# The residual of a graph convolution as a fourth filter, taken out of PSUM by VectorE

## The chip, the cores and the metric

The kernel runs on one core of a Trainium2 chip. The metric is the time of one execution on the device, in microseconds (us). TensorE (PE) multiplies, VectorE (DVE), ScalarE (ACT) and GpSimd (POOL) work elementwise, and SyncE (SP) issues the transfers. Each engine works its own queue in the order in which it is written; semaphores tie the queues together. Products land in PSUM, which has 8 banks of 128 partitions x 512 floats.

## The reference

The input is x, 16 batches x 256 nodes x 16 features x 16 time steps. A graph convolution with temporal and spatial attention comes first, then a linear attention layer, then a mixture of experts. The change lies in the end of the first block:

```
out = zeros
for k in range(3):
    r = einsum('mn,bmn,bmft->bnft', cheb[k], S, x)
    out = out + einsum('bnft,fo->bnot', r, Theta[k])
sg = relu(out)
tc = conv(sg, tw, kernel 1x3, pad 1) + tb        # over the time steps
res = einsum('bnft,of->bnot', x, rw) + rb
y = relu(res + tc)
y = (y - mean(y)) / sqrt(var(y) + 1e-5) * gamma + beta
```

S is a softmax that depends on the batch. Since the filters Theta work on the features only, the kernel applies them first, to x, and mixes the nodes afterwards.

## The kernel before

The batches go through in 8 pairs. Each pair runs through chains of named steps: `conv` (the graph convolution), `tail` (its normalisation), `attn`, `route` and `ffn` (the experts, 12 steps of a pair: gu, h, dn, w). One list, PROGRAM, puts the steps of all pairs in one order, and every engine issues its part of each step in that order (`run`). The list is written out by hand: OPENING for the pairs 0 to 2 of `conv`, BODY once per turn for the pairs 3 to 7, CLOSING for the end. In the list `+n` means n steps of the experts, which are to keep TensorE busy. `hot` steps are products whose result nobody uses; they fill gaps in the opening. `high` and `low` steps split the weights, on ScalarE and on VectorE.

The products of conv and attn land in a ring of four banks. Tile i of the whole list takes bank i % 4, and TensorE waits (`wait_bank`) until the tile four places before it was read out; READ_OUT says by which instruction of which engine.

The steps around the change, for a pair p and a batch b of it:
- xT: x, normalised and transposed, kept in `xT` (features and times on the partitions). M, prod, Epre, Eexp, Erep, lr, p2, sp, rv, st: the two attentions of the graph part. VectorE has small instructions in most of them; prod's is `te` (L931), ScalarE's tanh on it is L745, and Epre (L1304) needs that.
- Y0, Y1 (`filter_products`, L1237): strips of 32 rows of `xT` against the three filters, 16 products of 96 columns into four banks. ScalarE copies each bank to `y_s` (L740); that copy frees the bank.
- st (L1345), o0, o1 (L1355): transposes of the softmax, VectorE's products with cheb (L994), then the mixing of the nodes. ScalarE takes the relu to `sg` (L771).
- tc0, tc1: the bias as a product of `ones` and `bias_hl` (L1368), four residual products of `xT` with `residual_s` (L1373), four products of the time convolution with `tconv_s` (L1374, L1375). ScalarE takes the relu to `kept` (L776).
- z1: sums (L999), mean off (L1002), squares on ScalarE, products with gamma on GpSimd; z2: sums of squares, L1010, and three Newton steps on VectorE; z3: the rest.
- gn: statistics of x (L895) and one product (L1268).
- lg, r1 to r4, cb: the choice of experts. r4 is L1173 to L1181 on VectorE; cb (L1471) transposes its result, which then goes through DRAM to the experts.

In VectorE's queue the steps of BODY around Y0 read h, Y0, silu, r4, prod, cb, and around Y1 out0, V01, w, S10, Y1, h, st1, o0, o1, tc0, tc1, z1. In OPENING they read `0:M 0:Y0 2:gn 1:M`, then `0:Eexp 1:Y0 1:prod 2:xg`, then `0:tc1 0:high3 2:Y0 0:z1 1:rv1 2:prod 0:z2 0:low1 1:Y1 1:st1`.

Of the kernel before, what the change touches and what calls it, by code (L numbers as in the profile page):

```python
# [12 lines left out]
P = 128  # L13
B = 16
N = 256
T = 16
# [203 lines left out]
def graph_attention_moe(nc, x, out, small, consts, cheb, theta, residual, tconv, vsT, bsT, wqkvT, woT, gateT, upT, down):  # L220
    x_v = x.rearrange("(p b) (c n) f t -> p b n c (f t)", b=2, n=P)
    out_v = out.rearrange("(p b) (c n) f t -> p b n c (f t)", b=2, n=P)
    with ExitStack() as ctx:
# [17 lines left out]
        theta_s = sb("theta_s", [P, 3, 2, T])  # L241
        residual_s = sb("residual_s", [P, T, 8])
        tconv_s = sb("tconv_s", [P, T, 10])
        bias = sb("bias", [P, T])
        bias_h = sb("bias_h", [P, T], F32R)
        bias_hl = sb("bias_hl", [P, T], F32R)
# [11 lines left out]
        ones = sb("ones", [P, P], F32R)  # L258
# [158 lines left out]
        def fill(p, name):  # L417
# [4 lines left out]
            "M": "um sums left0 right1 left1", "prod": "te", "Epre": "emax esub", "Eexp": "e1 e2 e3 e4 e5 esum erec ET", "Erep": "EW WE", "p2": "pb0 pb1",  # L422
# [46 lines left out]
        for b in BI:  # L469
            READ_OUT["xT" + b] = [(conv_act, "xT" + b)]  # L470
            READ_OUT["p2_" + b] = [(conv_dve, "pb" + b)]
            READ_OUT["sp" + b] = [(conv_act, f"ex{b}1")]
            READ_OUT["st" + b] = [(conv_dve, f"A{b}2")]
            READ_OUT["o" + b] = [(conv_act, "sg" + b)]
            READ_OUT["tc" + b] = [(conv_act, "relu" + b)]
            READ_OUT["tok" + b] = [(attn_act, f"nm{2 * int(b) + 1}")]
            READ_OUT["tk" + b] = [(route_act, f"nm{2 * int(b) + 1}")]
            READ_OUT["xl" + b] = [(attn_dve, "lo" + b)]
            READ_OUT["xn" + b] = [(route_dve, "lo" + b)]
            READ_OUT["q" + b] = [(attn_dve, "q" + b)]  # L480
# [81 lines left out]
        PREP_POOL = 11  # L562
# [4 lines left out]
        def _(sp):  # L567
# [11 lines left out]
            sp.dma_start(residual_s[:, :, :], residual).then_inc(load["blocks"], 16)  # L579
# [65 lines left out]
        def _(pool):  # L645
# [4 lines left out]
            pool.memset(bias_hl[:, :].bitcast(F32), 0.0).then_inc(prep_pool, 1)  # L650
# [53 lines left out]
        def _(act):  # L704
# [11 lines left out]
            def front(p, name):  # L716
# [5 lines left out]
                if t is not None:  # L722
                    act_reads = name in ("xT0", "xT1", "lr", "o0", "o1", "tc0", "tc1", "xl0", "xl1", "xn0", "xn1", "kt", "q0", "q1", "k0", "k1", "v0", "v1")
                    if act_reads:
                        act.wait_ge(*filled_at(p, name))
                if name == "M" and p == 0:
                    act.wait_ge(prep_dve, 6)
                    act.wait_ge(prep_pool, 6)
                    act.activation(bias_h[:, :], bias[:, :], ACT.Copy).then_inc(prep_act, 1)
                    act.activation(bias_hl[64:65, :], bias[64:65, :], ACT.Copy).then_inc(prep_act, 1)  # L730
# [110 lines left out]
        def _(dve):  # L841
            def prepare():

                dve.wait_ge(load["small"], 16)
                dve.wait_ge(load["first"], 16)
                dve.tensor_scalar(ve_h[:, :, :], small_at("ve", T).unsqueeze(1).to_broadcast([T, 4, T]), 0.5, None, ALU.mult).then_inc(prep_dve, 1)
                dve.tensor_copy(iw1[:, 0:16], const_at("ident", T)[:, 0:16]).then_inc(prep_dve, 1)
                dve.tensor_copy(iw1[:, 16:17], small_at("w1", T)).then_inc(prep_dve, 1)
                dve.tensor_copy(iw1[:, 17:18], small_at("w1", T)).then_inc(prep_dve, 1)
                dve.wait_ge(prep_act, 1)  # L850
                dve.tensor_tensor(router[:, :, 1, :], small_at("router").rearrange("p (k e) -> p k e", k=2), router[:, :, 0, :].bitcast(F32), ALU.subtract).then_inc(prep_dve, 1)
                dve.tensor_tensor(bias[:, :], small_at("tb"), small_at("rb"), ALU.add).then_inc(prep_dve, 1)
                dve.tensor_scalar(ones[:, :], ident, 0.0, 1.0, ALU.mult, ALU.add).then_inc(prep_dve, 1)
# [28 lines left out]
            def front(p, name):  # L882
# [80 lines left out]
                if name == "lr" and p == 0:  # L963

                    dve.wait_ge(load["rest"], 16)
                    dve.wait_ge(prep_act, 3)
                    dve.wait_ge(prep_dve, 6)
                    dve.tensor_tensor(bias_hl[96:97, :], bias[96:97, :], bias_h[96:97, :].bitcast(F32), ALU.subtract).then_inc(prep_dve, 1)
# [238 lines left out]
        def _(pe):  # L1207
# [19 lines left out]
            def filter_products(p, name):  # L1227
# [29 lines left out]
            def front(p, name):  # L1257
# [32 lines left out]
                if name in ("Y0", "Y1"):  # L1290
                    if p == 0:
                        pe.wait_ge(load["blocks"], 48)
# [38 lines left out]
                if name in ("sp0", "sp1"):  # L1331
                    b = int(name[2])
                    if p == 0:
                        pe.wait_ge(prep_dve, 9)
# [25 lines left out]
                if name in ("tc0", "tc1"):  # L1360

                    b = int(name[2])
                    if p == 0:
                        pe.wait_ge(prep_dve, 8)
                        pe.wait_ge(prep_pool, 6)
# [224 lines left out]
```

## Time and profile before

| | |
|---|---|
| median of 3 runs | 949.14 us (947.37 to 950.04) |
| span of the profiled execution, first to last instruction | 943.2 us |
| TensorE busy | 896.8 us |
| VectorE busy | 604.5 us |
| ScalarE busy | 426.2 us |
| GpSimd busy | 210.3 us |

The profile is of one execution. Its own time is its span; the runs' times have some microseconds around the span (949.14 - 943.2 = 5.9). A step's busy time says nothing of whether it delays the end: for that one reads who waits for whom.

### The profile page before, as it was taken

Reading aid. Unit: us, or ns where it says so; the run is one execution under the profiler, and the core shown is the slowest. Engines: PE = TensorE matmul, PEld = TensorE weight load, DVE = VectorE, ACT = ScalarE, POOL = GpSimd, SP = SyncE. Lnnn points to the kernel's source line nnn. Section 1 sums busy time; section 2 is a strip of 40 time slices with the busy share of each in tenths; the row PEclk is TensorE's granted clock in tenths of the full one; section 3 lists DMA queues with packets and bytes.
Section 4 is the critical chain, followed back from the end, with each engine's and each line's share of the span. In section 5 each row is a group of like instructions: output and inputs, shape, how many; then the busy total and the mean of one; then the engine's idle time right before and its main releaser. Section 6 shows DMA issues by size and latency. Waiting matters only on the chain.

```text
span 943.2 us, 19688 instructions
## 1 busy us (share of the span) xinstructions
PE 896.8 (95%) x8000; PEld 799.1 (85%) x8000; DVE 604.5 (64%) x1615; ACT 426.2 (45%) x781; POOL 210.3 (22%) x183
## 2 busy tenths in 40 slices
PE   4898879999999999999999999999999999999997
PEld 3687658998988998898988989888888898988997
DVE  6637967677775379654786458853787537764522
ACT  2534534831674336552464425652366424622442
POOL 2004101233301142112411124021331123122232
PEclk9999999999999999999999999999999999999998
DMA  6000400111011100210002010020001100020121
GB/s 233 2 1 1 171 23 2 57 62 35 13 39 57 35 24 13 73 35 23 24 14 82 24 35 23 25 72 31 27 13 52 55 2 24 30 77 24 38 66 34
DMA packets 36249, 39.26 MB, mean 42 GB/s; under 512 B 3392, under 2 KB 32576, under 8 KB 36160
## 3 DMA queue, kind: packets, MB, share of 16 engines
q1 hardware_dynamic: 36160, 38.01, 12.7%
q8 instruction: 64, 1.05, 0.5%
q14 instruction: 25, 0.20, 0.1%
HBM read 33.02 MB, written 4.98 MB: 40 GB/s over the span
## 4 chain that ended last, share of the span: by engine, by line
PE 85%; DVE 6%; DMA 4%; ACT 2%; issue 2%; POOL 1%; SPq 0%; POOLq 0%; DVEq 0%
PE ring L1355 9%; PE d_ps L521 5%; PE g_ps L521 5%; PE d_ps L522 4%; PE d_ps L523 4%; PE g_ps L523 4%; PE g_ps L522 4%; PE u_ps L522 4%; PE u_ps L521 4%; PE u_ps L523 4%; PE ring L1223 4%; PE num L1252 3%; PE ring L1338 3%; PE ring L1455 3%; PE ring L521 3%; PE ring L523 2%
## 5 line engine op out<-in xcount | busy, mean ns | idle before, releaser
L699 POOL TENSOR_TENSOR hl<-hb,hh 128x512 fp32r<-128x512 f32 x96 | 126.7, 1320 | 480.0 <-ACT hh L836 480.0
L836 ACT ACTIVATE hh<-hb 128x512 fp32r<-128x512 f32 x96 | 60.6, 632 | 181.8 <-DVE hb L1195 169.4
L521 PE MATMUL d_ps<-hh,down_h 128*128 128x256 f32 x384 | 114.9, 299 | 5.1 <-POOL hl L699 5.1
L521 PE MATMUL g_ps<-normed_h,gate_h 128*128 128x256 f32 x352 | 107.4, 305 | 3.5 <-DVE hb L1190 3.5
L1190 DVE TENSOR_TENSOR hb<-sl,u_ps 128x512 f32<-128x512 f32 x88 | 60.2, 684 | 77.2 <-PE u_ps L523 35.9
L522 PE MATMUL d_ps<-hl,down_h 128*128 128x256 f32 x384 | 107.7, 280 | 0.0
L523 PE MATMUL d_ps<-hh,down_l 128*128 128x256 f32 x384 | 107.7, 280 | 0.0
L522 PE MATMUL g_ps<-normed_l,gate_h 128*128 128x256 f32 x352 | 99.8, 283 | 0.0
L523 PE MATMUL g_ps<-normed_h,gate_l 128*128 128x256 f32 x352 | 99.8, 283 | 0.0
L522 PE MATMUL u_ps<-normed_l,up_h 128*128 128x256 f32 x352 | 99.5, 283 | 0.0
L521 PE MATMUL u_ps<-normed_h,up_h 128*128 128x256 f32 x352 | 99.4, 283 | 0.0
L523 PE MATMUL u_ps<-normed_h,up_l 128*128 128x256 f32 x352 | 99.4, 282 | 0.0
L1082 DVE TENSOR_TENSOR shared<-ring,constants 128x512 f32<-128x512 f32 x128 | 79.4, 683 | 16.4 <-PE ring L1223 16.4
L521 PEld LDWEIGHTS d_ps<-hh,down_h 128*128 128x128 f32 x384 | 72.5, 189 | 16.5 <-POOL hl L699 8.2
L521 PEld LDWEIGHTS g_ps<-normed_h,gate_h 128*128 128x128 f32 x352 | 67.0, 190 | 13.3 <-issue 8.1
L522 PEld LDWEIGHTS d_ps<-hl,down_h 128*128 128x128 f32 x384 | 72.8, 190 | 0.4 <-issue 0.2
L523 PEld LDWEIGHTS d_ps<-hh,down_l 128*128 128x128 f32 x384 | 72.6, 189 | 0.0
L833 ACT ACTIVATE sl<-g_ps 128x512 f32<-128x512 f32 x88 | 52.7, 599 | 41.5 <-PE g_ps L523 41.2
L522 PEld LDWEIGHTS g_ps<-normed_l,gate_h 128*128 128x128 f32 x352 | 67.1, 191 | 1.5 <-issue 1.2
L523 PEld LDWEIGHTS g_ps<-normed_h,gate_l 128*128 128x128 f32 x352 | 67.0, 190 | 0.0
L521 PEld LDWEIGHTS u_ps<-normed_h,up_h 128*128 128x128 f32 x352 | 66.7, 189 | 0.0
L522 PEld LDWEIGHTS u_ps<-normed_l,up_h 128*128 128x128 f32 x352 | 66.6, 189 | 0.0
(413 smaller groups left out, 2092.5 us busy)
## 6 DMA issues: line engine op xcount, KB each, us to landing
weights_over_hidden<-weights_by_expert SPq DMA_DIRECT2D x128, 128.0 KB, 2.9
shared<-denominators_by_head SPq DMA_DIRECT2D x16, 256.0 KB
out_x<-kept SPq DMA_DIRECT2D x16, 256.0 KB, 2.2
x_s<-in_x SPq DMA_DIRECT2D x12, 256.0 KB, 3.6
raw_weights<-in_gateT SPq DMA_DIRECT2D x4, 384.0 KB, 6.6
raw_weights<-in_upT SPq DMA_DIRECT2D x4, 384.0 KB, 6.0
raw_weights<-in_down SPq DMA_DIRECT2D x4, 384.0 KB, 8.0
cheb_s<-in_cheb SPq DMA_DIRECT2D x3, 256.0 KB, 4.9
```

The costliest lines, as they stand in the source:

```text
L521: eng.matmul(ps, wh, xh, start=start, stop=False, **how)
L522: eng.matmul(ps, wh, xl, start=False, stop=False, **how)
L523: return eng.matmul(ps, wl, xh, start=False, stop=stop, **how)
L699: pool.tensor_tensor(hl[:, j % 2, :], hb, hh[:, j % 2, :].bitcast(F32), ALU.subtract).then_inc(*ffn_pool.mark(p, f"lo{j}"))
L833: act.activation(sl, gate_up(p, j)[0][:, :], ACT.Silu).then_inc(*ffn_act.mark(p, f"si{j}"))
L836: act.activation(hh[:, j % 2, :], hb, ACT.Copy).then_inc(*ffn_act.mark(p, f"hi{j}"))
L1082: dve.tensor_tensor(p_s[:, j, :].rearrange("p (h l) -> p h l", h=4), tile(p, n)[:, :].rearrange("p (h l) -> p h l", h=4), const_at("causal ...
L1190: dve.tensor_tensor(hb, sl, gate_up(p, j)[1][:, :], ALU.mult).then_inc(*ffn_dve.mark(p, f"h{j}"))
L1223: last = pe.matmul(tile(p, n)[:, 2 * c * P:(2 * c + 2) * P], k_f[rows, c, cols], q_eo[rows, :, c, cols], start=True, stop=True, tile_posit ...
L1252: last = pe.matmul(num[rows, c * L + lc * P:c * L + lc * P + P], v_s[:, b, lc, 4 * c + j, 16 * odd:16 * odd + 32], p_s[:, j, (2 * c + odd) ...
L1338: last = pe.matmul(t[:, kc * N:(kc + 1) * N], vs_s[:, jc, kc * P:(kc + 1) * P], g.th[:, b, jc, :], start=(jc == 0), stop=(jc == 1))
L1355: last = pe.matmul(t[:, c * N:(c + 1) * N], g.y_s[b][:, m, c, k], g.a_s[:, k, m, :], start=(k == 0 and m == 0 and c == 0), stop=(k == 2 an ...
```

## The change

The residual's weights become a fourth filter of the strip product, which now fills its four banks completely (128 columns per product). ScalarE still copies the three filters' parts of a bank to `y_s`. Behind it VectorE takes the fourth part, adds the bias and writes it to `kept`; that take frees the bank. The bias product and the residual products of tc go. VectorE adds what it kept to the bank of tc, in place, ahead of ScalarE's relu. The wait for the stored output of three pairs before moves from the relu to the first take. Some preparation goes: one transfer, a memset, two copies, two VectorE instructions.

```
-        theta_s = sb("theta_s", [P, 3, 2, T])
-        residual_s = sb("residual_s", [P, T, 8])
+        theta_s = sb("theta_s", [P, 4, 2, T])
...
-                READ_OUT[f"Y{b}_{j}"] = [(conv_act, f"y{b}{j}")]
+                READ_OUT[f"Y{b}_{j}"] = [(conv_dve, f"r{b}{j}")]
...
-                        act.activation(g.y_s[b].rearrange("p m c k s -> p (m c k) s")[:, :, 32 * j:32 * j + 32],
-                                       tile(p, n)[:, 0:384].rearrange("p (q s) -> p q s", s=32), ACT.Copy).then_inc(*conv_act.mark(p, f"y{b}{j}"))
+                        act.activation(g.y_s[b].rearrange("p m c k s -> p (m c) k s")[:, :, :, 32 * j:32 * j + 32],
+                                       tile(p, n)[:, :].rearrange("p (q k s) -> p q k s", k=4, s=32)[:, :, 0:3, :], ACT.Copy).then_inc(*conv_act.mark(p, f"y{b}{j}"))
...
                 if name in ("tc0", "tc1"):
                     b = int(name[2])
-                    if p >= 3:
-                        act.wait_ge(out_stored[p % 3], 32 * (p // 3))
+                    act.wait_ge(conv_dve.of(p), conv_dve.at(p, f"res{b}"))
                     act.activation(x1_at(p)[:, :, b, :], t[:, :].rearrange("p (m r) -> p m r", m=2), ACT.Relu).then_inc(*conv_act.mark(p, f"relu{b}"))
...
+                if name in ("Y0", "Y1"):
+                    b = int(name[1])
+                    if p == 0 and not b:
+                        dve.wait_ge(prep_dve, 6)
+                    if p >= 3:
+                        dve.wait_ge(out_stored[p % 3], 32 * (p // 3))
+                    for j, n in enumerate(banks_of(name)):
+                        dve.wait_ge(conv_act.of(p), conv_act.at(p, f"y{b}{j}"))
+                        by_k = tile(p, n)[:, :].rearrange("p (m c k s) -> p m c k s", m=2, c=2, k=4)
+                        dve.tensor_tensor(x1_at(p)[:, :, b, :].rearrange("p m (c s) -> p m c s", c=2)[:, :, :, 32 * j:32 * j + 32], by_k[:, :, :, 3, :],
+                                          bias[:, :, :].rearrange("p t o -> p (t o)").unsqueeze(1).to_broadcast([P, 2, 2 * T]).unsqueeze(1).to_broadcast([P, 2, 2, 2 * T]),
+                                          ALU.add).then_inc(*cv.mark(p, f"r{b}{j}"))
+                if name in ("tc0", "tc1"):
+                    b = int(name[2])
+                    dve.wait_ge(*filled_at(p, name))
+                    own(cv, p, f"r{b}3")
+                    by_o = t[:, :].rearrange("p (m o t) -> p m o t", m=2, t=T)
+                    dve.tensor_tensor(by_o, by_o, x1_at(p)[:, :, b, :].rearrange("p m (t o) -> p m o t", o=T), ALU.add).then_inc(*cv.mark(p, f"res{b}"))
...
-                            last = pe.matmul(tile(p, n)[:, q * 96:(q + 1) * 96], g.xT[rows, b, c, m * P:(m + 1) * P],
+                            last = pe.matmul(tile(p, n)[:, q * P:(q + 1) * P], g.xT[rows, b, c, m * P:(m + 1) * P],
...
-                    pe.matmul(by_o, ones[:, :], bias_hl[:, :].unsqueeze(1).to_broadcast([P, 2, T]).unsqueeze(3).to_broadcast([P, 2, T, T]),
-                              start=True, stop=False, skip_group_check=True)
                     for m in range(2):
                         cols = slice(m * P, (m + 1) * P)
-                        for c in range(2):
-                            pe.matmul(by_o[:, m, :, 8 * c:8 * c + 8], g.xT[:, b, c, cols], residual_s[:, :, :], start=False, stop=False, skip_group_check=True)
-                        pe.matmul(by_o[:, m, :, 0:9], g.sg[:, b, 0, cols], tconv_s[:, :, 1:10], start=False, stop=False, skip_group_check=True)
+                        pe.matmul(by_o[:, m, :, 0:9], g.sg[:, b, 0, cols], tconv_s[:, :, 1:10], start=(m == 0), stop=False, skip_group_check=True)
```

## Rows read from the trace of the kernel before

**Rows 1.** Windows: engine busy us (instructions), granted clock, DMA share, GB/s.
```profile
25.00:50.00 25.00, 21.37 (x183) 15.71 (x182) 15.60 (x46) 14.33 (x36) 0.00 (x0) 0.93 0.01 2
...
440.00:560.00 120.00, 117.99 (x1076) 105.17 (x1073) 80.42 (x216) 54.52 (x100) 29.21 (x24) 1.00 0.11 33
```

**Rows 2.** Chain of waits, one turn: start us, us, engine, tile, line, count with loads.
```profile
420.36 1.08 PE ring L1237 x32
421.43 1.01 PE num L1252 x32
...
433.61 0.44 PE ring L1373 x4
```

**Rows 3.** Source line L1068: duration in ns, min/median/max.
```profile
L1068 DVE TENSOR_SCALAR one_over_denominator<-ring x8: 281/286/292, 111.4 to 827.6; 128x128 f32<-128x128 f32 x8
```

**Rows 4.** Timeline of tc0, tc1: start us, us, engine, line, tiles, [idle before].
```profile
433.04 0.57 PE L1368 MATMUL ring<-bias_hl,ones 128*128 128x512 f32 x1
...
433.43 0.60 ACT L771 ACTIVATE filters<-ring 128x512 f32<-128x512 f32 x1 [4.58 <-PE ring L1355]
...
433.45 0.61 PE L1373 MATMUL ring<-residual_s,first 128*128 128x128 f32 x4
...
437.31 0.38 PE L521 MATMUL d_ps<-hh,down_h 128*128 128x256 f32 x1
...
437.61 0.60 ACT L776 ACTIVATE kept<-ring 128x512 f32<-128x512 f32 x1 [1.49 <-PE ring L1375]
...
438.90 1.15 PE L1223 MATMUL ring<-shared 32*128 32x256 f32 x16
```

**Rows 5.** Timeline behind Y0 in a turn of BODY.
```profile
490.61 0.22 DVE L1173 SCALAR_TENSOR_TENSOR pairs<-emark,sc 128x64 f32<-128x64 f32 x1
...
490.70 1.64 ACT L740 ACTIVATE filters<-ring 128x384 f32<-128x384 f32 x4 [1.44 <-PE ring L1237]
...
491.54 0.22 DVE L1181 TENSOR_TENSOR pairs<-pairs,wsum 128x64 f32<-128x64 f32 x1
...
492.30 0.60 PE L1471 MATMUL num<-constants,pairs 128*16 128x128 f32 x4
...
492.41 0.18 DVE L931 TENSOR_TENSOR conv_small<-ring,small_parameters 16x32 f32<-16x32 f32 x1 [0.65 <-PE ring L1298]
...
492.99 0.27 PE L1304 MATMUL ring<-conv_small,ve_h 16*64 16x32 f32 x2
```

**Rows 6.** Timeline of the opening behind Y0 of pairs 0 and 1.
```profile
18.36 1.41 DVE L895 BATCH_NORM_STATS2 conv_small<-x_s 128x6 f32<-128x256 f32 x4
19.08 1.64 ACT L740 ACTIVATE shared<-ring 128x384 f32<-128x384 f32 x4 [0.51 <-PE ring L1237]
...
20.72 0.36 PE L1268 MATMUL ring<-conv_small,constants 128*128 128x8 f32 x2 [1.71 <-ACT shared L740]
...
26.70 1.64 ACT L740 ACTIVATE raw_weights<-ring 128x384 f32<-128x384 f32 x4 [0.78 <-PE ring L1237]
...
27.54 0.18 DVE L931 TENSOR_TENSOR sl<-ring,small_parameters 16x32 f32<-16x32 f32 x1
```

**Rows 7.** Timeline of the opening, z1 of pair 0 to st1 of pair 1.
```profile
67.32 1.48 DVE L999 TENSOR_REDUCE shared<-kept 128x32 f32<-128x512 f32 x2
...
72.92 1.06 DVE L1010 TENSOR_SCALAR shared<-shared 128x64 f32<-128x64 f32 x1
...
73.39 0.66 PE L1345 MATMUL ring<-constants,raw_weights 128*128 128x128 f32 x4 [0.30 <-ACT raw_weights L740]
...
76.69 0.95 DVE L859 TENSOR_TENSOR wqkv_l<-raw_weights,wqkv_h 128x768 fp32r<-128x768 f32 x1
```

**Rows 8.** Timeline of the opening, Erep of pair 2.
```profile
91.49 1.06 PE L1311 MATMUL ring<-iw,first 16*128 16x17 f32 x8 [1.60 <-ACT shared L791]
```

**Rows 9.** Windows around a fall of the granted clock.
```profile
106.00:108.00 2.00, 0.69 (x5) 0.52 (x6) 1.93 (x4) 1.15 (x2) 0.00 (x0) 1.00 0.81 306
...
110.00:112.00 2.00, 2.00 (x20) 1.28 (x20) 1.65 (x4) 2.00 (x4) 0.00 (x0) 0.50 1.04 395
```

More of the change, by code:

```diff
@@ L217, with graph_attention_moe @@
 PLACE = {f: i for i, f in enumerate(FILLS)}
-def graph_attention_moe(nc, x, out, small, consts, cheb, theta, residual, tconv, vsT, bsT, wqkvT, woT, gateT, upT, down):
+def graph_attention_moe(nc, x, out, small, consts, cheb, theta, tconv, vsT, bsT, wqkvT, woT, gateT, upT, down):
     x_v = x.rearrange("(p b) (c n) f t -> p b n c (f t)", b=2, n=P)
@@ L240, in graph_attention_moe @@
         cheb_s = sb("cheb_s", [P, 3, 2, N])
-        theta_s = sb("theta_s", [P, 3, 2, T])
-        residual_s = sb("residual_s", [P, T, 8])
+        theta_s = sb("theta_s", [P, 4, 2, T])
         tconv_s = sb("tconv_s", [P, T, 10])
-        bias = sb("bias", [P, T])
-        bias_h = sb("bias_h", [P, T], F32R)
-        bias_hl = sb("bias_hl", [P, T], F32R)
+        bias = sb("bias", [P, 2, T])
         vs_s = sb("vs_s", [P, 2, N])
@@ L257, in graph_attention_moe @@
         down_h = sb("down_h", [P, CHUNKS, N], F32R)
-        ones = sb("ones", [P, P], F32R)
         over = sb("weights_over_hidden", [P, 2, 512])
@@ L421, in graph_attention_moe @@
             "gn": "bn0 bn1 bn2 bn3 ag0 ag1 ag2 ag3 msq m2 gm gsq gvar", "xg": "xg0 xg1 xg2 xg3",
-            "M": "um sums left0 right1 left1", "prod": "te", "Epre": "emax esub", "Eexp": "e1 e2 e3 e4 e5 esum erec ET", "Erep": "EW WE", "p2": "pb0 pb1",
+            "M": "um sums left0 right1 left1", "prod": "te", "Epre": "emax esub", "Eexp": "e1 e2 e3 e4 e5 esum erec ET", "Erep": "EW WE", "p2": "pb0 pb1", "Y0": "r00 r01 r02 r03", "Y1": "r10 r11 r12 r13", "tc0": "res0", "tc1": "res1",
             "sp0": "smax0", "sp1": "smax1", "rv0": "rinv0", "rv1": "rinv1", "st0": "A00 A01 A02", "st1": "A10 A11 A12"}), early("conv_by_dve"))
@@ L561, in graph_attention_moe @@
         ROUTED_DOWN = {2: 13, 3: 14, 4: 14, 5: 14}
-        PREP_POOL = 11
+        PREP_POOL = 10
         assert len(PIECES) == len(CHAINS["high"]) == len(CHAINS["low"])
@@ L578, in _ @@
             sp.dma_start(theta_s[:, :, :, :], theta).then_inc(load["blocks"], 16)
-            sp.dma_start(residual_s[:, :, :], residual).then_inc(load["blocks"], 16)
             sp.dma_start(tconv_s[:, :, :], tconv).then_inc(load["blocks"], 16)
@@ L649, in _ @@
                 pool.memset(r.ab[:, :, :], 0.0).then_inc(prep_pool, 1)
-            pool.memset(bias_hl[:, :].bitcast(F32), 0.0).then_inc(prep_pool, 1)
             pool.memset(gs[:, :, :], FILLER).then_inc(prep_pool, 1)
@@ L722, in front @@
                 if t is not None:
-                    act_reads = name in ("xT0", "xT1", "lr", "o0", "o1", "tc0", "tc1", "xl0", "xl1", "xn0", "xn1", "kt", "q0", "q1", "k0", "k1", "v0", "v1")
+                    act_reads = name in ("xT0", "xT1", "lr", "o0", "o1", "xl0", "xl1", "xn0", "xn1", "kt", "q0", "q1", "k0", "k1", "v0", "v1")
                     if act_reads:
@@ L726, in front @@
                 if name == "M" and p == 0:
[L727 to L730, printed above, removed]
+                    act.wait_ge(prep_pool, 2)
                 if name in ("xT0", "xT1"):
@@ L851, in prepare @@
                 dve.tensor_tensor(router[:, :, 1, :], small_at("router").rearrange("p (k e) -> p k e", k=2), router[:, :, 0, :].bitcast(F32), ALU.subtract).then_inc(prep_dve, 1)
-                dve.tensor_tensor(bias[:, :], small_at("tb"), small_at("rb"), ALU.add).then_inc(prep_dve, 1)
-                dve.tensor_scalar(ones[:, :], ident, 0.0, 1.0, ALU.mult, ALU.add).then_inc(prep_dve, 1)
+                dve.tensor_tensor(bias[:, :, :], small_at("tb").unsqueeze(1).to_broadcast([P, 2, T]), small_at("rb").unsqueeze(1).to_broadcast([P, 2, T]),
+                                  ALU.add).then_inc(prep_dve, 1)
             def split(i):
@@ L965, in front @@
                     dve.wait_ge(load["rest"], 16)
-                    dve.wait_ge(prep_act, 3)
-                    dve.wait_ge(prep_dve, 6)
-                    dve.tensor_tensor(bias_hl[96:97, :], bias[96:97, :], bias_h[96:97, :].bitcast(F32), ALU.subtract).then_inc(prep_dve, 1)
                     dve.wait_ge(load["graph"], 96)
@@ L1291, in front @@
                     if p == 0:
-                        pe.wait_ge(load["blocks"], 48)
+                        pe.wait_ge(load["blocks"], 32)
                     pe.wait_ge(conv_act.of(p), conv_act.at(p, f"xT{name[1]}"))
@@ L1333, in front @@
                     if p == 0:
-                        pe.wait_ge(prep_dve, 9)
+                        pe.wait_ge(prep_dve, 7)
                     pe.wait_ge(conv_act.of(p), conv_act.at(p, f"th{b}"))
@@ L1563 @@
     consts = _np.concatenate([c[n].astype(f32) for n in CONST], axis=1)
-    theta = _np.zeros((8, T, 3, 2, T), f32)
-    residual = _np.zeros((8, T, T, 8), f32)
+    theta = _np.zeros((8, T, 4, 2, T), f32)
     tconv = _np.zeros((8, T, T, 10), f32)
     for t in range(8):
-        theta[t, :, :, t % 2, :] = a["L0_conv_Theta"].transpose(1, 0, 2)
-        residual[t, :, :, t] = a["L0_conv_rw"].T
+        theta[t, :, 0:3, t % 2, :] = a["L0_conv_Theta"].transpose(1, 0, 2)
+        theta[t, :, 3, t % 2, :] = a["L0_conv_rw"].T
         tconv[t, :, :, t:t + 3] = a["L0_conv_tw"][:, :, 0, ::-1].transpose(1, 0, 2)
-    theta, residual, tconv = (v.reshape((P,) + v.shape[2:]) for v in (theta, residual, tconv))
+    theta, tconv = (v.reshape((P,) + v.shape[2:]) for v in (theta, tconv))
     given = {
-        "x": a["x"], "small": small, "consts": consts, "cheb": a["L0_conv_cheb"], "theta": theta, "residual": residual, "tconv": tconv,
+        "x": a["x"], "small": small, "consts": consts, "cheb": a["L0_conv_cheb"], "theta": theta, "tconv": tconv,
         "vsT": a["L0_conv_V_s"].T, "bsT": a["L0_conv_b_s"][0].T,
```

3 lines of the change are left out of this document (removed).

## The prediction

> **What bounds the kernel now.** I read the page's busy times first (the table above): TensorE is busy nearly all the span, ScalarE and VectorE are far from it. The windows of the span then show that this is an average over two different kernels: between 440 and 560 us TensorE works 98% of the time (117.99 of 120 us), between 25 and 50 us only 85%, with VectorE at 15.60 of 25 [rows 1]. So in the steady part (pairs 3 to 7 of the graph stage, one each 111.12 us, five times) a microsecond taken off TensorE is a microsecond gained, unless TensorE then waits; in the opening (pairs 0 to 2) the end is set by chains that go from engine to engine in the order written in OPENING, and VectorE's place in them matters as much as its speed. Every engine works its queue in order, so a VectorE instruction that waits for ScalarE holds up everything written behind it. That is what I look for in the timelines [rows 5 to 8].
>
> **TensorE loses work in tc.** Per tc step the change takes away one 512-column bias product and four residual products, each of which is two passes; four passes last 0.44 us in the chain of waits [rows 2], so eight are 0.89. The pass behind the bias product starts 0.41 us after it [rows 4]; part of that is the end of the product before, which stays, so its share is between 0 and 0.41, and I take half, 0.21. Together 1.1 us a step, 2.2 us a pair, 17.6 us over 8 pairs. That is nearly the whole possible gain: of the preparation, a few small instructions on three engines and a transfer go, 0 to 0.5 us once, and I take 0.
>
> **The fourth filter on TensorE.** The strip product goes from 96 to 128 moving columns, in 8 groups of four side by side. Its step takes 1.08 us in the chain; the attention's weighting has the same 8 groups, 128 columns wide, and takes 1.01 [rows 2]. So 96 columns do not pay by the column today, and a residual pass with 128 weight columns and 128 moving ones takes 0.11, which is 0.89 for 8 [rows 2]. Bounds for the 16 steps: 0 below, 0.36 x 16 = 5.8 us above, if all 1.08 grew with the columns. I take 0, the nearest rows being those 128 wide.
>
> **ScalarE** still moves 384 elements of each bank, now in blocks of 96; four take 1.64 us today [rows 5]. No row has that pattern out of PSUM; the 128x512 eviction takes 0.60 [rows 4], which bounds the one of 384 from above: 0 to 0.1 more each, and I see no reason for a gain. I take 0.
>
> **VectorE gains** eight takes of 128 elements a pair (nearest: a 128x128 read of PSUM, 0.286 us median [rows 3]) and two adds of 512 (nearest: two reductions of 512 in 1.48, or 0.7 each [rows 7]; no row writes its result back to PSUM, so 0.6 to 1.0). That is 8 x 0.28 + 2 x 0.7 = 3.6 us a pair, 29 us in all. Its busy time allows for that. The question is what stands behind them. The wait for the stored output, which moves to the first take, costs nothing: the store of three pairs before is issued about a sixth of a turn ahead of Y0.
>
> **Steady part, Y0.** In VectorE's queue the order is h2, Y0, r4, prod. Today Y0 has nothing there: r4 (L1173 to L1181) starts at 490.61 and ends at 491.76, before TensorE wants its result for cb at 492.30 [rows 5]. ScalarE's four evictions run from 490.70 to 492.34. With the change the fourth take starts at 492.38 and ends at 492.66; r4 starts at about 492.60, which is 1.99 us later, and ends at 493.75. TensorE can start cb (L1471) at 493.80 instead of 492.30. The te addition (L931), 492.41 today, comes behind r4 at 493.76, the tanh follows, and Epre (L1304) is ready at about 494.33 instead of 492.99. So TensorE loses 1.35 us, and nothing filled that time for it. The weights' way through DRAM starts at cb and shifts with TensorE, so its stalls stay what they are. The same rows come back five times, first at 268 and last at 713 us.
>
> **Steady part, Y1.** Here the takes run while VectorE is idle. But the bank that st1 needs is free only after the first take, 0.3 us behind ScalarE, of which about 0.1 is covered: 0.2 us.
>
> **Steady part, tc.** o1 ends at 433.4, its relu at 434.03 [rows 4]. tc0 is then done at 434.2, so tc1 doesn't wait. Between tc and z1 comes a hop: product, add 0.7, relu 0.60. The relu of tc1 ends 1.5 us behind the last product where it is 0.9 today; S11 takes that bank 1.6 us behind it (437.31 to 438.90, [rows 4]), so it just fits. The sums and subtractions, the masks of S11 and V11 come 0.7 us later against TensorE, with slack of 0.8 to 0.9. I put 0.1 us here. A pair: -2.2 + 1.35 + 0.2 + 0.1 = -0.55; five pairs: **-2.7 us**.
>
> **Opening, Y0 of pairs 0 and 1.** In the queue of VectorE pair 2's statistics stand behind pair 0's Y0. They start at 18.36 today; ScalarE's evictions end at 20.72 [rows 6], so the last take ends at 21.03 and the statistics start at 20.96: 2.6 us later, and TensorE's next product (L1268, 20.72) waits for them. The row already shows TensorE idle there; it is the same chain, so nothing absorbs it. In pair 1, the te addition at 27.54 stands behind takes that end 0.3 us after 28.34 [rows 6]: 1.1 us more. Sum **+3.7**. Pair 0's Y1: as in the steady part, with nothing over it, **+0.3**.
>
> **Opening, 66 to 80 us.** This is the costly place. VectorE's queue reads: tc1 of 0, Y0 of 2, z1 of 0, rv1 of 1, prod of 2, z2 of 0, low1, Y1 of 1, st1 of 1. Today z1 starts at 67.32, and TensorE transposes st1 of 1 at 73.39, while z2 and low1 run on VectorE until 77.64 beside the next products [rows 7]. With the change:
> - tc0 and tc1 of pair 0 end earlier on TensorE, but st0 of 1 waits for ScalarE's scaling, and the relu of tc1 comes through VectorE: Y0 of 2 starts 0.2 us earlier, not 2.2.
> - z1 now stands behind the takes of Y0 of 2, which end at 71.15. It starts at 71.1 and ends at 73.8 (2.67 us, as today).
> - te of 2 ends at 74.1. The squares and GpSimd's two products come behind the subtractions; L1010, which today ends with GpSimd's second product (72.92 + 1.06 = 73.98, [rows 7]), ends at about 76.1.
> - From L1010's end to low1's end it is 3.66 us today (73.98 to 77.64): 79.8.
> - Only then comes the take of the first bank of Y1 of 1, which ends at 80.05. st1 uses that bank, so TensorE starts it at 80.1 where it was 73.39.
> That is **+6.7 us**, the 0.2 included. TensorE stands still for some 4 us of it. Today the eviction alone frees the bank; so the cover of z2 by o0 and o1 is lost.
>
> **Opening, the rest.** tc of 1: TensorE waits at Erep of 2 (L1311, 1.60 us idle today, [rows 8]) for a normalisation behind relu1 and shift; of 2.2 us I keep **-0.8**. Y1 of 2: **+0.3**. tc of 2: **-2.2**. Opening: 3.7 + 0.3 + 6.7 - 0.8 + 0.3 - 2.2 = **+8.0 us**.
>
> **The clock.** Today the granted clock is 1.00 at 106 to 108 us, while TensorE works 0.69 of 2 us, and 0.50 at 110 to 112 [rows 9]; between 25 and 50 us the mean is 0.93, which at 25 x 0.07 is 1.75 us of lost work in one fall to 1.2 GHz [rows 1]. The idle stretch of 4 us before st1 of pair 1, where the products of o0 run without a gap today, should bring one more: **+1.7 us** (bounds 0 and 3.4). The Trainium skill says the same in general (TensorE: Matmul & The Clock Gate, section on HAM oscillation): a wait that is long enough drops the array to half clock, and the loss is half of the throttled time. By that rule as well, one more fall costs 1.7; it speaks against this change, whose sum without it would be 5.3.
>
> **Sum** against the profiled span of 943.2 us: +8.0 - 2.7 + 1.7 = +7.0, so 950.2. The runs' median, 949.14, is 5.9 above the span, which I keep: **956 us**, 0.7% slower.
>
> **Rivals.**
> - *The opening gives most of it back.* If the stretch at 66 to 80 costs no more than the late normalising (1.5 us instead of 6.7) and the clock doesn't fall: 2.8 - 2.7 = 0, 949. For it: the opening has idle time on every engine. Against: the waits are in the order of the queues, which the diff doesn't touch. 0.18.
> - *TensorE's saving carries.* The other side: the bound is TensorE's work, and VectorE's takes are covered. Place: tc, 8 x 2.2 = 17.6 us. If nothing waits it is 931; it decides from the point where the waits of Y0, 1.35 each, and the opening's 11 us lose half, 940 to 946. For it: TensorE's 98% in the steady part [rows 1]. Against: r4 has 0.54 us of slack at cb, and comes 1.99 later [rows 5]. 0.12.
> - *VectorE and the columns cost more.* If the strip product pays by its columns (5.8 us), the takes in four-level patterns are slower or the clock falls twice: 962. For it: no row has these patterns. Against: 128 columns side by side take 1.01 us [rows 2], and the takes read rows of 32 neighbours. 0.10.
> - My forecast: 0.60, its own range 952 to 959.
>
> **How the numbers follow.** About 0.3%, or 2.8 us, is what a measurement of this kernel tells from no change. Slower: the forecast 0.60 and the last rival 0.10. Same: 0.18. Faster: 0.12. The range 946 to 963 leaves the saving that carries fully below and a double clock loss above.
>
> **What would show it.** After: L1173 starts behind the fourth take in every turn and TensorE idles 1.3 to 1.5 us at L1471 or Epre, the turn being 110.6 us instead of 111.12; in the opening the statistics of pair 2 start near 21.0, and TensorE idles at least 3 us before st1 of pair 1, near 84 us in the new trace, with z2 and low1 on VectorE. The steps are wrong if the strip product lasts over 1.2 us, if cb starts on time, or if st1 of 1 comes within 6 us of the old 73.4. If the turn is shorter than 110 us, the prediction is wrong about Y0.

## The result, and the profile after

| | before | after |
|---|---|---|
| median (runs) | 949.59 us (4; 947.37 to 950.96) | 957.25 us (4; 956.72 to 960.29) |
| span of the profiled execution | 943.2 us | 955.0 us |
| TensorE busy | 896.8 us | 891.2 us |
| VectorE busy | 604.5 us | 636.1 us |
| ScalarE busy | 426.2 us | 425.4 us |

The changed kernel is slower: ratio 1.0094, 95% interval 1.0069 to 1.0118. A second set, told below, gives 1.0085 (1.006 to 1.011). The forecast was 956, range 946 to 963. One execution of a later kernel took 1301 us at a mean granted clock of 0.64 and is left out of its numbers (experiment 6). TensorE is busy 5.6 us less, VectorE 32 us more, and the span is 11.8 us longer, so TensorE's idle time grew by 17.4 us. (TensorE's busy time shrinks by less than the work that was taken off it, since products last longer at the lower clock; see below.) The waits of TensorE, summed over the span after; the columns are the engine's group of products, what it waited for, us in total, times, longest:

```profile
PE num L1469 <- DVE pairs L1186: 7.0, 5, 1.4
...
PE ring L1273 <- DVE conv_small L894: 4.3, 1, 4.3
PE ring L1350 <- DVE kept L972: 3.5, 2, 3.2
...
PE ring L1316 <- ACT shared L781: 3.1, 1, 3.1
...
PE d_ps L517 <- POOL hl L693: 2.7, 2, 2.2
PE ring L1242 <- ACT kept L766: 2.6, 1, 2.6
PE ring L1242 <- DVE conv_small L921: 2.6, 1, 2.6
PE ring L1228 <- ACT kept L766: 2.3, 5, 0.5
```

The first row is cb in the five turns (L1469 was L1471); L1273 is the product of pair 2's statistics (was L1268), L1350 is st (was L1345), L1228 is S (was L1223), L1242 the strip product (was L1237). L972 is the new take, L980 the new addition, L766 the relu. The waits of TensorE before had no row for cb, none for st behind `kept` and none for S behind the relu. Two rows of before shrink in the profile after (to 2.7 and 0.7 us), which I had not expected:

```profile
PE d_ps L521 <- POOL hl L699: 5.1, 7, 2.2
...
PE ring L1318 <- DVE conv_small L962: 2.1, 5, 0.7
```

**One turn at cb**, timeline of the kernel after (start, length, engine, line, what, idle before). It answers to [rows 5]:

```profile
503.76 1.64 ACT L731 ACTIVATE filters<-ring 128x384 f32<-128x384 f32 x4 [1.45 <-PE ring L1242]
504.35 1.37 DVE L972 TENSOR_TENSOR kept<-ring,bias 128x128 f32<-128x128 f32 x4 [0.59 <-ACT filters L731]
505.64 0.21 DVE L1178 SCALAR_TENSOR_TENSOR pairs<-emark,sc 128x64 f32<-128x64 f32 x1
506.56 0.22 DVE L1186 TENSOR_TENSOR pairs<-pairs,wsum 128x64 f32<-128x64 f32 x1
506.70 0.17 DVE L921 TENSOR_TENSOR conv_small<-ring,small_parameters 16x32 f32<-16x32 f32 x1
506.84 0.60 PE L1469 MATMUL num<-constants,pairs 128*16 128x128 f32 x4 [1.40 <-DVE pairs L1186]
```

r4 starts 1.88 us behind the first eviction, where it was 0.09 ahead of it; TensorE stands idle 1.40 us. The evictions still take 1.64 us, a take 0.29.

**tc**, the same view, answering to [rows 4]:

```profile
448.14 0.41 PE L1373 MATMUL ring<-tconv_s,filters 128*128 128x144 f32 x2
...
448.63 0.41 PE L1373 MATMUL ring<-tconv_s,filters 128*128 128x144 f32 x2
...
449.08 2.08 DVE L980 TENSOR_TENSOR ring<-ring,kept 128x512 f32<-128x512 f32 x2 [5.47 <-PE ring L1373]
...
450.14 0.60 ACT L766 ACTIVATE kept<-ring 128x512 f32<-128x512 f32 x1 [1.45 <-DVE ring L980]
...
451.19 0.60 ACT L766 ACTIVATE kept<-ring 128x512 f32<-128x512 f32 x1 [0.45 <-DVE ring L980]
451.93 0.93 PE L1228 MATMUL ring<-shared 32*128 32x256 f32 x12 [0.45 <-ACT kept L766]
```

One addition takes 1.04 us, not 0.7. The second relu ends at 451.79, and S11 waits for it.

**The opening at the statistics of pair 2 and at st1 of pair 1**, the same view, answering to [rows 6] and [rows 7]:

```profile
20.28 1.37 DVE L972 TENSOR_TENSOR kept<-ring,bias 128x128 f32<-128x128 f32 x4 [1.62 <-ACT shared L731]
21.57 1.39 DVE L885 BATCH_NORM_STATS2 conv_small<-x_s 128x6 f32<-128x256 f32 x4
...
23.92 0.36 PE L1273 MATMUL ring<-conv_small,constants 128*128 128x8 f32 x2 [4.30 <-DVE conv_small L894]
```

```profile
81.25 1.44 DVE L972 TENSOR_TENSOR kept<-ring,bias 128x128 f32<-128x128 f32 x4 [3.25 <-ACT filters L731]
...
82.60 1.27 DVE L1004 TENSOR_REDUCE shared<-kept 128x32 f32<-128x512 f32 x2
...
85.06 0.16 DVE L921 TENSOR_TENSOR conv_small<-ring,small_parameters 16x32 f32<-16x32 f32 x1
...
85.28 2.21 POOL L673 TENSOR_TENSOR kept<-kept,small_parameters 128x512 f32<-128x512 f32 x2 [13.14 <-ACT shared L776]
...
85.37 1.69 PE L1242 MATMUL ring<-theta_s,raw_weights 32*128 32x128 f32 x32 [2.55 <-DVE conv_small L921]
...
86.49 1.04 DVE L1015 TENSOR_SCALAR shared<-shared 128x64 f32<-128x64 f32 x1
...
90.25 0.95 DVE L849 TENSOR_TENSOR wqkv_l<-raw_weights,wqkv_h 128x768 fp32r<-128x768 f32 x1
...
91.11 0.87 DVE L972 TENSOR_TENSOR kept<-ring,bias 128x128 f32<-128x128 f32 x4
...
91.45 0.90 PE L1350 MATMUL ring<-constants,raw_weights 128*128 128x128 f32 x3 [3.24 <-DVE kept L972]
```

The chain of the prediction is there link by link: takes of Y0 of 2, z1 (L1004), the te addition (L921), L1015, low1 (L849), and only then the take whose bank st1 needs.

**The clock.** Windows of the kernel after; columns as in [rows 1]:

```profile
25.00:50.00 25.00, 21.51 (x140) 13.94 (x132) 12.97 (x48) 8.81 (x20) 0.96 (x1) 0.67 0.00 1
440.00:560.00 120.00, 117.35 (x1031) 105.04 (x1029) 79.97 (x213) 53.58 (x98) 28.02 (x23) 1.00 0.11 33
...
86.00:96.00 10.00, 6.76 (x35) 5.10 (x32) 5.58 (x18) 2.29 (x7) 4.45 (x4) 0.50 0.01 2
```

At 25 to 50 us the granted clock is 0.67, where it was 0.93, and behind the idle stretch before the late strip product of Y1 it is 0.50 for 10 us. Between 20 and 900 us the stretches at 1.2 GHz add up to 37.5 us after, against 10.2 in the profile of before.

### The profile page after: what moved, and what is told of

The parts are those of the page before. It is cut to its first block, busy times and chain, and to the rows that moved or that the text cites. A ratio compares the mean times of both kernels' runs of the same rounds, so it can differ in the third digit from the quotient of the medians.

```text
span 955.0 us, 19489 instructions
## 1 busy us (share of the span) xinstructions
PE 891.2 (93%) x7856; PEld 788.0 (83%) x7856; DVE 636.1 (67%) x1693; ACT 425.4 (45%) x779; POOL 209.7 (22%) x182
## 4 chain that ended last, share of the span: by engine, by line
PE 82%; DVE 9%; ACT 4%; issue 2%; DMA 1%; POOL 1%; SPq 0%; POOLq 0%; DVEq 0%; ACTq 0%
PE ring L1360 8%; PE g_ps L517 5%; PE d_ps L517 5%; PE g_ps L519 4%; PE g_ps L518 4%; PE u_ps L519 4%; PE u_ps L518 4%; PE u_ps L517 4%; PE d_ps L519 4%; PE d_ps L518 4%; PE ring L1228 4%; PE num L1257 3%; PE ring L1453 3%; PE ring L1343 3%; PE ring L519 3%; PE ring L517 3%
## 5 line engine op out<-in xcount | busy, mean ns | idle before, releaser
L1195 DVE TENSOR_TENSOR hb<-sl,u_ps 128x512 f32<-128x512 f32 x88 | 60.1, 683 | 59.5 <-PE u_ps L519 38.4
L517 PEld LDWEIGHTS g_ps<-normed_h,gate_h 128*128 128x128 f32 x352 | 66.5, 189 | 13.2 <-issue 8.1
L519 PEld LDWEIGHTS u_ps<-normed_h,up_l 128*128 128x128 f32 x352 | 66.2, 188 | 0.0
```

The source lines that it names most:

```text
L517: eng.matmul(ps, wh, xh, start=start, stop=False, **how)
L519: return eng.matmul(ps, wl, xh, start=False, stop=stop, **how)
L1195: dve.tensor_tensor(hb, sl, gate_up(p, j)[1][:, :], ALU.mult).then_inc(*ffn_dve.mark(p, f"h{j}"))
```

## The experiments

All ratios are to the kernel before, run on the same chip, with 95% intervals. Differences to the changed kernel (957.25 us) are between chips; the kernel before has medians of 947.1 to 949.6 us there, so they are good to some 2 us. A "step" is the start of one of TensorE's steps in one trace less its start in another, and what that difference changes by from the step ahead of it.

**1. The columns alone.** The kernel before with 128 columns and the block copy; the fourth part of a bank is filled and read by nobody. Experiments 3, 4, 5 and 8 are built on this kernel: they have 128 columns in all pairs and keep the old preparation.

```
-  act.activation(y_s ..., tile(p, n)[:, 0:384] ...)
+  act.activation(y_s ..., tile(p, n)[:, :] ... [:, :, 0:3, :])
-  pe.matmul(tile(p, n)[:, q * 96:(q + 1) * 96], ...)
+  pe.matmul(tile(p, n)[:, q * P:(q + 1) * P], ...)
```

> The kernel before, with the fourth filter in the strip product (128 columns instead of 96) and ScalarE's copy in blocks, but nobody reads the fourth part; the residual stays in tc. Theory (the strip product is not paid by its columns): same as before within 1 us, its step still 1.08 us. Rival (it pays by its columns): 16 steps x 0.36 = 5.8 us more.

Measured: 948.68 us (10 runs) against 948.71 (23), ratio 1.0005 (0.9989 to 1.0022). The fourth filter costs TensorE nothing; by the upper bound of 5.8 us the ratio would be 1.006.

**2. TensorE's saving alone.** The changed kernel without VectorE's takes and additions, so without residual and bias; ScalarE's copy frees the bank.

```
-  READ_OUT[f"Y{b}_{j}"] = [(conv_dve, f"r{b}{j}")]
+  READ_OUT[f"Y{b}_{j}"] = [(conv_act, f"y{b}{j}")]
-  (the takes and the additions)
```

> The changed kernel without VectorE's takes and adds; this leaves out the residual and the bias of y. ScalarE's copy frees the bank again. Theory (TensorE's saving is real, VectorE's waits eat it): 16 to 19 us faster than before, about 932. Rival (part of the loss is in the product or in ScalarE's copy): only 5 to 12 us faster.

Measured: 928.7 us (4 runs), ratio 0.9789 (0.9758 to 0.9819), 20 us faster, a little over the 16 to 19 expected. The saving is real, though some 3 of the 20 us come from a small transfer that is quicker in three turns (experiment 11). VectorE's share of the change costs 28.5 us where it is busy 32 us longer; here the transfer is no part of the difference, since it is quick in three turns in both kernels.

**3. and 4. The steady part and the opening alone.** Old way in pairs 0 to 2, new in 3 to 7; and the reverse.

```
+  NEW = {3, 4, 5, 6, 7}      (4: {0, 1, 2})
...
+  if name in ("Y0", "Y1") and p in NEW:   (takes)
+  if name in ("tc0", "tc1") and p in NEW: (addition)
+  residual_here = p not in NEW            (TensorE's products)
```

> Pairs 0 to 2 in the old way (residual and bias in tc), pairs 3 to 7 in the new one. Theory (the loss is all in the opening, each steady turn gains about 1.25 us net: 2.2 saved, 1.5 lost at cb, 0.5 at S11, 1.1 of older waits absorbed): 5 to 7 us faster than before, 943. Rival (the takes cost everywhere, the profile after was a lucky one): no faster than before.

> The reverse: pairs 0 to 2 in the new way, pairs 3 to 7 in the old one. Theory: the whole loss, 7.7 + 6 = 13 to 15 us slower than before, 963. Rival (the steady part has a share in the loss): at most 8 us slower.

Measured: steady part alone 944.57 (12 runs), 0.9961 (0.9941 to 0.9981): 3.7 us faster, where 5 to 7 were expected. Opening alone 955.89 (6 runs), 1.0074 (1.0051 to 1.0096): 7 us slower, where 13 to 15 were expected. The number is the rival's (at most 8); its reason, a loss in the steady part, is not seen in experiment 3, though that gain too holds the quick transfers told below. Both were misses: the expected numbers came from the profile of before, which is a quick execution (span 943.2 us; the 27 runs of that kernel in experiment 11 have spans of 942.4 to 949.0), and from a turn that in experiment 4 is shorter, though its steady part is the old one. Experiment 11 shows what goes with the shorter turn. It also means that neither result is the change's alone: that transfer is quick in four of five turns in experiment 3 and in all five in experiment 4, in none before.

**5. The takes of Y0 behind r4.** Experiment 3 with one step moved: for pairs 3 to 7 the takes of Y0 stand at prod, ahead of te.

```
-  "prod": "te",  "Y0": "r00 r01 r02 r03"
+  "prod": "r00 r01 r02 r03 te"
```

> The kernel with the new way in pairs 3 to 7 only, and the takes of Y0 moved in VectorE's queue from Y0 to behind r4, ahead of prod's addition. Theory (the wait at cb comes from r4 standing behind the takes, and the falls of the clock around 273, 495 and 717 us come from that wait): cb on time, 1.3 us a turn less, no half clock in the steady part, together 8 to 12 us faster than the same kernel with early takes, so 932 to 937. Rival (the takes cost wherever they stand, and the clock falls by itself): 943 to 945 as with early takes.

Measured: 938.77 us (6 runs), 0.9889 (0.9861 to 0.9918), the fastest kernel here that leaves nothing out, 5.8 us below experiment 3. The direction is the theory's, the size is not: 8 to 12 us and 932 to 937 were expected. Timeline of it at cb:

```profile
492.84 0.23 DVE L1225 TENSOR_TENSOR pairs<-pairs,wsum 128x64 f32<-128x64 f32 x1
492.99 1.03 DVE L952 TENSOR_TENSOR kept<-ring,bias_wide 128x128 f32<-128x128 f32 x4
493.65 0.32 PEld L1518 LDWEIGHTS num<-constants,pairs 128*16 128x16 f32 x4
493.65 0.61 PE L1518 MATMUL num<-constants,pairs 128*16 128x128 f32 x4
```

cb has no wait. Windows behind cb in experiment 3 (first fence) and 5 (second):

```profile
495.00:499.00 4.00, 4.00 (x17) 3.45 (x17) 2.58 (x11) 3.27 (x6) 0.00 (x0) 0.57 0.13 40
```

```profile
495.00:499.00 4.00, 4.00 (x30) 3.73 (x29) 3.19 (x11) 3.80 (x7) 0.00 (x0) 1.00 0.14 43
```

In experiment 3 the granted clock falls to 1.2 GHz behind the wait at cb in three of five turns, for 3.4 us each; in 5 it stays at 2.4 GHz in all. The Trainium skill (TensorE: Matmul & The Clock Gate, "A second HAM failure mode: psum-queue depth-cycling") tells of another kernel in which frequent small idles between groups of products made the clock swing between its two levels. The traces here agree in part: one wait of 1.4 us at cb can be enough, but is not each time. Over all profiles, six have that wait (experiments 3, 6, 7, 10 and the two of after), and the clock falls within 2 us of cb in 9 of their 30 turns; it falls in none of the 40 turns of the eight profiles without it.

**6. The order of the opening.** The changed kernel with z1 of 0 ahead of Y0 of 2, and z2 of 0 and low1 behind Y1 of 1.

```
-  0:tc1 0:high3 2:Y0 0:hot11 0:z1 0:hot12 1:rv1 2:prod 0:z2 0:low1 1:Y1 0:hot13 1:st1
+  0:tc1 0:z1 0:high3 2:Y0 0:hot11 0:hot12 1:rv1 2:prod 1:Y1 0:hot13 0:z2 0:low1 1:st1
```

> The changed kernel with two moves in the written order of the opening, nothing else: z1 of pair 0 goes ahead of Y0 of pair 2, and z2 of pair 0 and low1 go behind Y1 of pair 1. Theory (TensorE waits at st1 of pair 1 because the take that frees its bank stands behind z2 and low1): the 6 us between Y0 of pair 2 and st1 of pair 1 shrink below 2, the kernel gains 4 to 8 us, 949 to 953. Rival (the opening is short of VectorE time as such): no gain, 957.

Measured: 951.79 us (9 runs; 952.37 with the one of 1301 us), 1.0044 (1.0017 to 1.0071), 5.5 below the changed kernel (4.9 with it). Timeline at st1 of pair 1:

```profile
86.02 1.44 DVE L960 TENSOR_TENSOR kept<-ring,bias 128x128 f32<-128x128 f32 x4 [1.90 <-ACT raw_weights L719]
86.37 0.66 PE L1338 MATMUL ring<-constants,raw_weights 128*128 128x128 f32 x4 [0.30 <-DVE kept L960]
```

The wait of 3.24 us is 0.30, and st1 starts at 86.37 instead of 91.45. So the chain at 66 to 80 us is an effect of the order in VectorE's queue.

**7. Work in the waits, to hold the clock.** The changed kernel with 17 unused products ahead of gn of 2, Y1 of 1 and st1 of 1.

> The changed kernel with 17 more unused products on TensorE, 5 ahead of gn of pair 2, 4 ahead of Y1 of pair 1, 8 ahead of st1 of pair 1, where it stands idle: the waits stay. Theory (beside the waits, the half clock that follows them costs, some 34 us of it in the opening): the half-clock windows behind them go, 3 to 7 us faster than the changed kernel, 950 to 954. Rival (only the waits cost, the clock falls wherever it falls): 957 or more.

Measured: 956.26 us (9 runs), 1.0077 (1.0051 to 1.0102). A miss: 950 to 954 were expected. The fall at 86 us is gone, but others come at 128, 173 and 292 us, and between 20 and 900 us 44.4 us are at 1.2 GHz where the two profiles of after have 37.5 and 41.0. Not distinguishable from the changed kernel; filling these three waits did not put the clock right.

**8. Everything moved.** New way and late takes in all pairs, both moves of experiment 6, and gn, M and xT1 ahead of Y0 of 0.

> The new way in all pairs, with the late takes of Y0, and with gn, M and xT1 ahead of Y0 of pair 0 and the two moves of z1 and z2. Theory (every loss is one of place in the queues): the opening costs at most 2 us against the kernel before and the steady turns gain 2 us or more each: 932 to 938. Rival: the hop through VectorE in the opening costs anyway, 940 to 946.

Measured: 947.86 us (12 runs), 0.999 (0.9971 to 1.001). A miss by 10 us, and above the rival's 940 to 946 too. A steady turn takes 108.9 us where its small transfer is quick (experiment 11), 1.3 less than the old way with the same (110.1 to 110.3 in experiment 4), for 2 or more expected. The larger part of the miss lies in the opening, for which at most 2 us were expected: cb of the first steady turn starts at 280.2 us, against 270.0 and 274.2 in the two profiles of before. The one move that I followed passes most of its gain on: hot3 starts at 24.92 us where it starts at 26.78 in experiment 6, but only 1.2 of these 1.9 us are left at Epre of pair 0, where TensorE now waits 1.25 us and not 0.62. How the rest divides between takes and clock was not tried; a stretch of 13.7 us at half clock, here from 33.3 us, is in the profile of experiment 1 as well (from 30.1 us), whose opening is the old one.

**9. Late takes for pairs 3 to 7 and the order of experiment 6**, new way in all pairs.

> The changed kernel in all eight pairs, with both repairs that helped alone: for pairs 3 to 7 VectorE's takes of Y0 stand behind r4, ahead of prod's addition, and in the opening z1 of pair 0 stands ahead of Y0 of pair 2 and its z2 and low1 behind Y1 of pair 1. If the costs are waits that add up (my theory), the two gains add to the changed kernel's 957.3: 4.9 from the opening's order and 5.8 from the late takes, so 946 to 947, ratio about 0.997. Rival: the gains hang together through the granted clock, which falls elsewhere once the waits are gone; then it lies at 950 or more, ratio 1.001 or above.

Measured: 944.06 us (12 runs), 0.9958 (0.9939 to 0.9977), 13.2 below the changed kernel where the two gains add to 11.3, and 2 us under the expected 946 to 947. Within what chips differ by, they add; the rival's 950 is out.

**10. Without the addition in tc.** The relu reads the bank of tc, so residual and bias are left out.

```
-  dve.tensor_tensor(by_o, by_o, x1_at(p)..., ALU.add)
-  act.wait_ge(conv_dve.of(p), conv_dve.at(p, f"res{b}"))
+  act.wait_ge(conv_dve.of(p), conv_dve.at(p, f"r{b}3"))
```

> The changed kernel without VectorE's two additions in tc: ScalarE's relu reads the bank of tc directly, so the residual and the bias are left out of the result; the eight takes stay. The step offsets of the kernel with all of VectorE's part left out give the additions some 0.5 us a turn at S11 and 0.7 to 1.1 at two places of the opening. If the rest of VectorE's 28 us is the takes' (my theory), this comes 4 to 6 us under the changed kernel: 951 to 953, ratio 1.002 to 1.004. Rival 1: the hop through VectorE between tc and its relu is half the cost: 943 or less. Rival 2: it is hidden: 956 to 958, and S11 waits as before.

Measured: 950.43 us (12 runs), 1.0015 (0.9999 to 1.0032), 6.8 below the changed kernel, a little over the 4 to 6 expected. S11 starts 0.53 us earlier per turn. Of VectorE's 28.5 us the additions have 6.8, and the takes the rest, if the two add.

**11. and 12. Both kernels again**, unchanged, for a second profile.

> The kernel before, unchanged, for a second profile. In its first one the small transfer of the routing weights to DRAM took 2.83 to 3.05 us from its issue to the issue of the reads behind it, in all five turns, and a turn took 111.2 us; in the kernel with the old way in pairs 3 to 7 it took 1.60 and the turn 110.2. My theory: the transfer has two durations whatever the kernel, so turns with 1.6 last 110.1 to 110.3 here too and those with 2.8 or more 111.1 to 111.4, and the granted clock's long stretch of 13.7 us at half speed, missing from the first profile, may be there. Rival: in this kernel the transfer is always the longer one, since the extra products of tc shift it; then all turns stay at 111.2 and the change itself gains the 1 us a turn.

> The changed kernel, unchanged, for a second profile and more times. My theory: turns in which the routing weights' write takes 1.6 us last 109.9 to 110.1, those with 2.6 or more about 1 us more; TensorE waits 1.4 us at cb in every turn and 3 us before st1 of pair 1 again, while the stretches at half clock lie elsewhere than in the first profile. Time 956 to 958. Rival: the waits move with the clock, and the one before st1 of pair 1 is below 2 us in this execution.

Measured: 947.91 us (10 runs), ratio to before 1.0002 (0.9982 to 1.0021), and 955.5 us (8 runs), 1.0085 (1.006 to 1.011). My theory of chance fell, and so did half of the rival. In the second profile of after the waits come again, 1.4 us at cb in five turns and 3.5 us ahead of st1 of pair 1, and so do the stretches at half clock: all six lie within 2 us of their places in the first one, against my expectation that they would move. The write of the routing weights (`comb`, 32 KB) took 2.7 to 3.3 us in all five turns of before again, and in after it took 1.60 in the first three and 2.7 in the last two, as in the first profile: it goes with the kernel. But not with tc's products: with the old tc it is 1.60 in all five turns of experiment 4. The DMA view between its issue and that of the reads behind it shows what goes with it. Before, 604.8 to 608.3 us (queue, kind: packets, MB, share; then the write's time to landing):

```profile
q1 hardware_dynamic: 32, 0.03, 4.6%
q8 instruction: 1, 0.02, 1.9%
...
weights_by_expert<-comb SPq DMA_DIRECT2D x1, 32.0 KB, 3.0
```

The kernel of experiment 4, 508.2 to 510.2 us:

```profile
q1 hardware_dynamic: 32, 0.03, 7.5%
...
weights_by_expert<-comb SPq DMA_DIRECT2D x1, 32.0 KB, 1.6
```

Of six writes in each of the 14 profiles, the 31 that took 2.39 to 3.51 us all have a packet of queue 8, a block of 16 KB of instructions, beside them, the 53 that took 1.58 to 1.62 have none. What a late write costs shows in the old way's turns: 111.2 to 111.5 us each before, 110.10 to 110.26 in experiment 4, so 1.0 to 1.3 us. It goes with the length of the write: in experiment 1, with writes of 3.1 to 3.3 us, a turn takes 111.7 to 112.0.

## Why the prediction was right, point by point

**Direction and size: right, the size in part by luck.** Forecast 956, measured 957.25 and 955.5. The waits that were forecast are there, but the span was put 4.8 us too short (950.2 for 955.0), and what was added for the way from span to time 4.1 us too long; the two cancel.

**The fourth filter and ScalarE's pattern at 0: right** (experiment 1; a strip step keeps its length within 0.03 us, the four evictions their 1.64).

**tc's saving of 2.2 us a pair: right.** In the steps of the trace it comes as 0.66 at tc0, 1.11 at tc1 and 0.44 behind it.

**Y0, 1.35 us a turn: right in place and size.** cb comes 1.47 us later in each of the five turns [rows 5], in experiment 5 not at all. **Y1, 0.2 us: too large.** The difference to before grows by less than 0.1 us from Y1 to st1.

**tc's hop, 0.1 us: too small.** An addition that writes back to PSUM takes 1.04 us (999 to 1061 ns in 16), above the upper end of my 0.6 to 1.0. The relus come later and S11 waits 0.45 us: 0.5 a turn. "It just fits" [rows 4] was argued with a duration from the wrong kind of row, two reductions that don't write to PSUM. The addition also reads and writes in rearranged order (features and times swapped); no run tells which of the two makes it slow.

**The steady turn: a missing term.** By its own terms a turn changes by -2.2 + 1.47 + 0.5 = -0.2 us, not -0.55. The turns with the quick write bear that out: 110.10 to 110.26 us in the old way, 109.90 to 110.13 in the new. But the turns of before had the late write in all five (5 to 6 us, hidden in the 111.12), and after has it in two. So the steady part gained 3.9 us in the trace (the difference to before falls from 15.8 at 195 us to 11.9 at 773 us) where 2.7 was forecast. The sign I had announced as proof against Y0, a turn under 110 us, came, and Y0 was right all the same: the test mixed two causes.

**Opening, a, statistics: right.** 2.62 us for 2.6. Their start is 21.57 for 21.0; the 0.6 was there ahead of Y0. **b**, te of 1: 0.53 for 1.1.

**Opening, 66 to 80 us: right in mechanism and size.** The steps Y0 of 2, Y1 of 1 and st1 of 1 lose 1.41, 1.85 and 3.46 us, 6.7 in all, for a forecast of 6.7 [rows 7]; experiment 6 takes 5 of them away. st1 starts at 91.45 and not near 84: what was late before it and the clock lie on top.

**Opening, the rest.** Erep of 2 waits 3.1 us where it waited 1.60 [rows 8] (3.0 in experiment 2): of tc of 1 some 0.7 us are kept, for a forecast of 0.8. Missed was the relu of tc0 of 0, which comes through VectorE's addition: 1.06 us at st0 of 1 (0 in experiment 2).

**The clock, +1.7: the term that was mis-sized.** I put one fall of 3.4 us. The two profiles of before have 10.2 and 23.9 us at 1.2 GHz ahead of 200 us, the two of after 34.1 and 37.5. The increase is not the chance of a single profile: among the runs of experiments 11 and 12, the mean granted clock is 0.985 to 0.995 in 27 runs of before and 0.974 to 0.983 in 8 of after, which is on average 22 us more at 1.2 GHz. It comes with VectorE's part in the opening: without that part (experiment 2) the runs lie at 0.985 to 0.992, with it in the opening alone (experiment 4) at 0.977 to 0.986. In the first profile of after the clock falls at 24.4 us behind the wait of 4.30 us, at 79.0 behind one of 2.63 and at 85.8 behind one of 2.55. In cost, by an estimate: TensorE is busy 30 us at half clock ahead of 200 us, against 10 and 23 in the profiles of before, and half of that is lost, so 4 to 10 us more than before. After is 15.8 and 11.6 us behind them at 195 us; that leaves 6 to 8 us for the waits of the opening, of which I had forecast 8.0. The estimate is rough: by it the two profiles of before are 6 us apart, and at 195 us they are 4.2 apart. Experiment 7 shows that filling three waits doesn't bring the clock back. Experiment 4 agrees with the total: with the 5 us or more that its quick writes gain it, it makes 12 us, of forecast 9.7.

**The bridge to the median was wrong in kind.** I kept 5.9 us between span and time. The profiled execution of after took 956.8 us for a span of 955.0, so 1.8; the remaining 4 are that the profile of before caught a quick execution. The sum stood against that one and needed +11.8 us of it, against the median +7.7; the forecast +7.0 matches the second only.

**The rivals.** That TensorE's saving carries (0.12) is out with what it needs: 20 us are there in experiment 2, and VectorE's takes eat them. That the opening gives it back (0.18) is out by experiment 4. Of the last (962, 0.10), the columns cost nothing, but a dearer VectorE instruction and a second loss to the clock are in the result.

## What to carry to other kernels

- Work moved from a full engine to one that is half idle is paid by its place in the second engine's queue: the same takes cost 1.47 us a turn ahead of r4 and nothing behind it, and that choice was worth 6 us over five turns, three falls of the clock behind the wait included (experiments 3 and 5).
- Freeing a buffer later is a dependency of its own: read off the queue of the engine that now frees it, down to the next instruction that needs the buffer.
- Before a difference of 1 us a turn is explained by the change, take a second profile of each kernel and look at the small transfers on the path, and compare the mean granted clock of all runs: a new wait can cost as much behind it as while it lasts (1.4 us at cb, and half of 3.4 us at 1.2 GHz where the clock falls).

## What the runs showed of the hardware

- A 32 KB write to DRAM takes 1.60 us, or 2.4 to 3.5 when a block of instructions of queue 8 is fetched at the same time (53 and 31 writes, without exception). Where the fetch falls goes with the program: the same turns have it in both profiles of before, and in both of after. Why it moves from kernel to kernel was not tried; that it depends on the number of TensorE's instructions ahead of it is a guess.
- 32 passes on 32 rows each, four side by side, take as long with 128 moving columns as with 96: 1.17 us in all and 1.15, the next step starting 1.08 us after theirs to within 0.03.
- An in-place 128x512 addition on PSUM takes 1.04 us on VectorE; a product of two tiles with one in PSUM and the result in SBUF 0.69 (L1195), an eviction on ScalarE 0.60.
- A small VectorE instruction that meets a GpSimd product is stretched to the end of that product. In pair 0 L1010 (L1015 after), 64 elements a partition, takes 1.06 us before and 1.04 after and ends some 0.05 us behind GpSimd's second product (73.98 and 73.93 us before, 87.53 and 87.49 after); in the seven other pairs no GpSimd product is beside it, and it takes 0.19 to 0.20.
- The granted clock fell within 2 us behind a TensorE wait of 1.4 us in 9 of 30 cases; in 40 turns of the same step without the wait it never fell.
